# One program of four blocks: keys of the causal attention made inside the recurrence's steps

## What is computed

```python
h_t  = GRU(h_{t-1}, x_t)                       # 256 steps, h_0 = cond
q, k, v = h @ Wq + bq, h @ Wk + bk, h @ Wv + bv   # 16 heads of 128
w    = softmax(q @ k.T / sqrt(128) + causal_mask)
x1   = x + (w @ v) @ Wo + bo
# conditioned attention: 16 heads of 16
xn   = rms_norm(x1, g) * (1 + scale) + shift   # scale, shift from cond
o    = softmax(rms_norm(q2) @ rms_norm(k2).T / 4) @ v2
y    = o + o @ W_out
out  = x1 + moe_ffn(y)     # 16 experts, 4 per position, and a shared one
```

## Time and profile of the kernel before

| | |
|---|---|
| median of 3 runs | 1055.14 us (1053.57, 1055.14, 1122.17) |
| profiled execution | 1052.69 us, its span 1050.9 us |
| PE, PEld busy | 933.1 us (89%), 698.3 us |
| DVE, ACT, POOL busy | 675.3, 530.9, 538.2 us |
| granted TensorE clock, mean of the span | 0.773 |

### The profile page before, as it was taken

One profiled execution on the slowest core, in us unless ns is written; L12 is line 12 of the kernel. 1 busy time (PEld: TensorE's weight loads), 2 busy tenths in 40 slices (PEclk: granted clock), 3 DMA queues, 4 the chain that ended last, 5 costly groups with the idle time before them and its releaser, 6 DMA issues. The chain is left out here.

```text
span 1050.9 us, 33951 instructions
## 1 busy us (share of the span) xinstructions
PE 933.1 (89%) x13640; PEld 698.3 (66%) x13640; DVE 675.3 (64%) x2501; ACT 530.9 (51%) x1781; POOL 538.2 (51%) x1183
## 2 busy tenths in 40 slices
PE   3889989899898998778999999857787999999997
PEld 3777777777777777666888888634343656665664
DVE  5866666666666666677777777667682666665665
ACT  3544444444444444455777777647665333233332
POOL 1266666666666666653555555257100655655652
PEclk8555555555555555578999999989799899999999
DMA  7100000000000000020110100010000133343441
GB/s 274 43 4 3 3 3 3 4 2 4 3 4 2 4 3 3 3 85 1 32 32 32 31 32 2 2 39 1 2 1 1 46 109 105 119 128 107 121 126 41
DMA packets 12744, 40.91 MB, mean 39 GB/s; under 512 B 2070, under 2 KB 3864, under 8 KB 12204
## 3 DMA queue, kind: packets, MB, share of 16 engines
q1 hardware_dynamic: 12588, 38.74, 11.5%
HBM read 37.36 MB, written 1.11 MB: 37 GB/s over the span
## 5 line engine op out<-in xcount | busy, mean ns | idle before, releaser
L423 POOL COPY gp<-hq 128x16 f16<-128x16 f16 x256 | 69.0, 269 | 174.6 <-DVE hq L413 174.6
L306 ACT ACTIVATE r_scan<-gr 128x8 f32<-128x8 f32 x256 | 46.3, 181 | 180.3 <-PE gr L218 180.3
L218 PEld LDWEIGHTS gr<-hq,w_two 128*128 128x128 f16 x1024 | 47.3, 107 | 115.1 <-DVE hq L408 109.9
L398 DVE TENSOR_REDUCE z_sum<-gz 128x8 f32<-128x16 f32 x256 | 44.8, 175 | 121.2 <-PE gz L218 120.5
L432 POOL TENSOR_TENSOR q_part<-q_raw,q_part 128x64 f16<-128x64 f32 x238 | 111.4, 468 | 19.2
L218 PE MATMUL gr<-hq,w_one 128*128 128x4 f16 x2048 | 117.6, 166 | 0.0
L218 PE MATMUL gr<-hq,w_two 128*128 128x4 f16 x1024 | 68.6, 172 | 51.6 <-DVE hq L408 28.8
L273 PE MATMUL gq<-gp,wq_part 128*128 128x64 f16 x1428 | 114.4, 237 | 0.0
L1735 POOL TENSOR_SCALAR w_hi<-wf_ffn 128x512 f16<-128x512 f32 (+1 forms) x56 | 29.6, 529 | 162.3 <-POOLq L985 75.1
L922 POOL TENSOR_SCALAR probs<-probs,rinv 128x128 f32<-128x128 f32 (+1 forms) x128 | 52.9, 425 | 111.9 <-DVE rinv L812 111.9
L430 POOL CAST q_part<-q_raw 128x64 f16<-128x64 f32 x238 | 109.0, 458 | 0.0
(11 more groups left out here) (237 smaller groups left out, 2733.6 us busy)
## 6 DMA issues: line engine op xcount, KB each, us to landing
wf_ffn<-in_wf SPq DMA_DIRECT2D x28, 384.0 KB, 3.2
raw_attn<-in_pairs SPq DMA_DIRECT2D x8, 770.0 KB, 5.2
cw_of<-cw_rows SPq DMA_DIRECT2D x9, 512.0 KB, 3.7
shared<-in_wq SPq DMA_DIRECT2D x1, 2056.0 KB, 12.1
cw_of<-cw_rows SPq DMA_DIRECT2D x4, 448.0 KB, 3.6
cw_of<-cw_rows SPq DMA_DIRECT2D x4, 384.0 KB, 3.5
cw_of<-cw_rows SPq DMA_DIRECT2D x4, 320.0 KB, 3.6
xT<-in_xT SPq DMA_DIRECT2D x1, 1024.0 KB, 7.6
```

What stands on the lines that cost most here:

```text
L218: mm = pe.matmul(out, w[:, j, rows], src, start=False, stop=False, skip_group_check=True)
L306: nc.scalar.activation(r_scan[:, 2::3], R[bp][:, k * 8:(k + 1) * 8], ACT.Sigmoid, scale=1.0 / GS).then_inc(t_in, 1)
L423: nc.gpsimd.tensor_copy(gp[:, :, :, :, t].rearrange("p q j b -> p q (j b)"), hq[:, nxt, :, 2::3]).then_inc(h_stored, 1)
```

## The change

**Recurrence.** Wk (2 MB) and its bias are loaded after wq. In steps 8 to 23 POOL splits one head's Wk, after the copy of the state and before the queries. From step 16, each step makes the keys of one head for the 16 positions before (6 matmuls of 64 columns, L300 of after) between the products and the queries; ACT reads out the high part (`k_made`) between the tanh and `q_raw`, and DVE makes the rest after the state's low part and before the next z. After 8 steps SP writes `k_made` to a buffer in DRAM, `k_kept`, by two DMAs. DVE waits for the copy of one step earlier ahead of z, PE no longer in each step.

**Attention.** Keys are made only for the last 16 positions, once a head (6 matmuls of 64 columns); the others of each head come back from `k_kept` (480 KB, one head ahead), so that the scores' moving operand is read in runs of 16. Values come in half batches, one group of 6 matmuls in each of the first 56 units. An exponential waits only for its own half of the maxima. `oT` has three buffers, and the projection lags by three units.

**Conditioned attention.** The q/k product alternates between two banks; the turned rows of the last two tiles alternate between two banks; the banks of the scores are 3, then 4, then 5. The batch product comes after the values, and the second shifted tile earlier. The feed-forward part is unchanged. Semaphores are merged to make room, and the raw weights of the recurrence share a buffer with the split Wk.

The core of the diff:

```diff
+        raws = sb("raws", [P, 6 * J * D + J * B * T])
+        whh, wih = (raws[:, n * J * 3 * D:(n + 1) * J * 3 * D].rearrange("p (j n) -> p j n", j=J)
+                    for n in range(2))
+        xT = raws[:, 6 * J * D:6 * J * D + J * B * T].rearrange("p (j b t) -> p j b t", j=J, b=B)
+        wk_part = raws[:, 0:H1 * J * P].bitcast(FP16).rearrange("p (w h n) -> p w h n", w=2, h=H1)
...
             sp.dma_start(wq, dram["wq"]).then_inc(loaded["wq"], 16)
+            sp.dma_start(bk[:], dram["bk"]).then_inc(loaded["wk"], 16)
+            sp.dma_start(wk, dram["wk"]).then_inc(loaded["wk"], 16)
...
+            for n in range((T - QB) // KSET):
+                first = n * KSET % H1
+                sp.wait_ge(k_lo, (n + 1) * KSET)
+                for q in range(2):
+                    sp.dma_start(k_kept[first:first + KSET, :, q, n * KSET // H1, :].rearrange("h p n -> p h n"),
+                                 k_made[:, n % 2, q]).then_inc(k_out[n % 2], 16)
...
-                if t:
+                if blk and k == 0:
                     pe.wait_ge(h_stored, t)
+                if blk:
+                    n_key = t - QB
+                    if t == QB + 1:
+                        pe.wait_ge(emb_act, 4)
+                    if t < 2 * QB:
+                        pe.wait_ge(wk_ready, k + 1)
+                    if queries_before(t):
+                        pe.wait_ge(q_read, queries_before(t))
+                    elif n_key >= 2:
+                        pe.wait_ge(k_lo, n_key - 1)
+                    for j in range(J):
+                        for w, g in ((1, 0), (0, 0), (0, 1)):
+                            mm = pe.matmul(q_bank[1 - t % 2][:, B * QB:2 * B * QB]
+                                           .rearrange("p (b t) -> p b t", b=B),
+                                           wk_part[:, w, k, j * P:(j + 1) * P],
+                                           gp[:, g, j, :, (blk - 1) * QB:blk * QB],
+                                           start=(j == 0 and w == 1), stop=(j == J - 1 and g == 1))
+                    mm.then_inc(k_psum, 1)
                 if query_of(t):
                     h, c = query_of(t)
                     m = queries.index(t)
-                    if m == 0:
-                        pe.wait_ge(emb_act, 4)
+                    pe.wait_ge(k_lo, t - QB)
                     if m < H1:
                         pe.wait_ge(wq_ready, c + 1)
                     if m >= 2:
                         pe.wait_ge(q_split, m - 1)
                     for j in range(J):
                         for w, g in ((1, 0), (0, 0), (0, 1)):
-                            mm = pe.matmul(q_bank[m % 2][:, 0:B * QB].rearrange("p (b t) -> p b t", b=B),
+                            mm = pe.matmul(q_bank[t % 2][:, 0:B * QB].rearrange("p (b t) -> p b t", b=B),
...
+                if t >= QB:
+                    n_key = t - QB
+                    group, place = n_key // KSET, n_key % KSET
+                    if n_key == 0:
+                        act.wait_ge(bk_ready, 1)
+                    if place == 0 and group >= 2:
+                        act.wait_ge(k_out[group % 2], 32 * (group // 2))
+                    act.wait_ge(k_psum, n_key + 1)
+                    nc.scalar.activation(k_made[:, group % 2, 0, place, :],
+                                         q_bank[1 - t % 2][:, B * QB:2 * B * QB], ACT.Identity,
+                                         bias=bk_scaled[:, k:k + 1]).then_inc(k_hi, 1)
...
+                if t >= 2:
+                    dve.wait_ge(h_stored, t - 1)
                 dve.wait_ge(z_psum, t + 1)
...
+                if t >= QB:
+                    n_key = t - QB
+                    group, place = n_key // KSET, n_key % KSET
+                    dve.wait_ge(k_hi, n_key + 1)
+                    nc.vector.scalar_tensor_tensor(
+                        out=k_made[:, group % 2, 1, place, :], in0=q_bank[1 - t % 2][:, B * QB:2 * B * QB],
+                        scalar=bk_scaled[:, k:k + 1], in1=k_made[:, group % 2, 0, place, :],
+                        op0=ALU.add, op1=ALU.subtract).then_inc(k_lo, 1)
...
                 pool.wait_ge(h_two, t + 2)
                 nc.gpsimd.tensor_copy(gp[:, :, :, :, t].rearrange("p q j b -> p q (j b)"),
                                       hq[:, nxt, :, 2::3]).then_inc(h_stored, 1)
+                if KSPLIT <= t < KSPLIT + H1:
+                    h = t - KSPLIT
+                    if h == 0:
+                        pool.wait_ge(loaded["wk"], 32)
+                        pool.wait_ge(w_ready, 1)
+                        pool.wait_ge(inputs_ready, 4)
+                        pool.wait_ge(x_ready, B)
+                    else:
+                        pool.wait_ge(wk_ready, h)
+                    nc.gpsimd.tensor_scalar(wk_part[:, 0, h], wk[:, h], KS, 0.0, ALU.mult, ALU.add)
+                    nc.gpsimd.tensor_scalar(wk_big[:], wk[:, h], KS, 0.0, ALU.mult, ALU.add) \
+                        .then_inc(wk_written, 1)
+                    pool.wait_ge(wk_written, h + 1)
+                    nc.gpsimd.tensor_tensor(wk_part[:, 1, h], wk_big[:], wk_part[:, 0, h],
+                                            ALU.subtract).then_inc(wk_ready, 1)
+                if t == KSPLIT + H1:
+                    pool.wait_ge(wk_ready, H1)
                 if query_of(t):
                     h, c = query_of(t)
                     m = queries.index(t)
...
+        kh = sb("kh", [P, 2, 2, H1, B * QB], FP16)
...
-            return 2 * (h + 1) + b // 2 if 0 <= u < units and b % 2 == 0 and h + 1 < H1 else None
+            return h + 1 if 0 <= u < units and b == 0 and h + 1 < H1 else None
...
-            return B * (pr + 1) + 2 * e + b // 2 if 0 <= u < units and b % 2 and pr + 1 < pairs else None
+            i, pr = u % (2 * B), u // (2 * B)
+            return (pr + 1, i // TC, i % TC) if 0 <= u < units and pr + 1 < pairs else None
...
+            def load_keys(h):
+                sp.dma_start(kh[:, h % 2, :, 0:H1 - 1, :], k_kept[h][:, :, 0:H1 - 1, :]).then_inc(k_in[h % 2], 16)
+
+            sp.wait_ge(k_out[0], 16 * (T - QB) // KSET)
+            load_keys(0)
+            load_keys(1)
...
+                sp.wait_ge(s_psum, B * (h - 1))
+                load_keys(h)
...
-                                       w_part["k"][:, h // 2 % 2, w, rows],
-                                       gp[:, g, j, 2 * half:2 * half + 2, :],
+                        mm = pe.matmul(last_keys(bank).rearrange("p (b t) -> p b t", b=B),
+                                       w_part["k"][:, h // 2 % 2, w, rows], gp[:, g, j, :, T - QB:T],
...
-                                       kh[:, e, k, b, 0:(tc + 1) * P], start=(m == 0), stop=(m == 2))
+                                       kh[:, e, k].rearrange("p a (b r) -> p b a r", b=B)[
+                                           :, b, 0:(tc + 1) * P // QB, :],
...
+            for u in range(units + 3):
                 if u + 1 < units:
                     h, b, _, _ = unit(u + 1)
                     if u + 1 == B * (H1 - 2):
                         pe.wait_ge(q_split, len(left_sets))
-                    pe.wait_ge(k_ready, 2 * h + b // 2 + 1)
-                    if value_group(u - 2) is not None:
-                        pe.wait_ge(v_ready, value_group(u - 2) + 1)
-                    if key_group(u - 2) is not None:
+                    if b == 0:
+                        pe.wait_ge(k_in[h % 2], 16 * (h // 2 + 1))
+                        pe.wait_ge(k_ready, h + 1)
+                    if value_group(u - 2):
+                        pe.wait_ge(v_ready, values_to(*value_group(u - 2)))
+                    if key_group(u - 2):
                         pe.wait_ge(k_ready, key_group(u - 2) + 1)
                     scores(u + 1)
-                if u >= 2:
-                    pe.wait_ge(oT_ready, u - 1)
-                    if (u - 2) % (2 * B) == 0:
-                        pe.wait_ge(w_split["o"], splits("o", (u - 2) // (2 * B)))
-                    projected(u - 2)
+                if u >= 3:
+                    pe.wait_ge(oT_ready, u - 2)
+                    if (u - 3) % (2 * B) == 0:
+                        pe.wait_ge(w_split["o"], splits("o", (u - 3) // (2 * B)))
+                    projected(u - 3)
...
+                    if u >= 2:
+                        pe.wait_ge(oT_ready, u - 1)
...
+                if key_group(u):
+                    h = key_group(u)
+                    pe.wait_ge(least_ready, 2 * (u + 2))
+                    if h // 2:
+                        pe.wait_ge(w_split["k"], splits("k", h // 2))
+                    keys(h, S[(u + 1) % 2])
+                if value_group(u):
+                    pr, b, sc = value_group(u)
+                    pe.wait_ge(least_ready, 2 * (u + 2))
+                    pe.wait_ge(w_split["v"], splits("v", pr))
+                    values(pr, b, sc, S[(u + 1) % 2][:, 0:2 * DH1]).then_inc(v_psum, 1)
...
-                act.wait_ge(least_ready, u + 1)
```

(29 more changed lines are left out.)

367 lines of the change are left out of this document (195 added, 172 removed).

## The result

Four executions of the changed kernel have a median of 1044.91 us (1041.69 to 1046.54) against 1054.84 us before; the ratio is 0.9905, with a 95% interval from 0.988 to 0.993. One execution of the kernel before, 1122.17 us, fell in a slow state of the chip and is left out of the ratio. The change is faster by about 10 us, not by the 26 that were forecast. The profiled execution took 1041.69 us, with a span of 1039.9.

A forecast was written before the change was run, and what follows sets the result against it. It took a chain of dependent instructions to bound the recurrence and PE the attention. 1052.7 + 10 (splitting Wk) - 28 (attention) - 6 (conditioned attention) = 1028.7, so 1029 us; own range 1019 to 1040, wider range 1014 to 1046.

The forecast's parts named there:

- The keys in the steps: Recurrence, 240 steps: the keys' work on PE, ACT and DVE fits their idle time, price 0.
- Its new wait for the state's copy: Recurrence, DVE ahead of z: the wait concerns the step before last and is long met, price 0.
- Splitting Wk: Recurrence, steps 8 to 23: POOL's split of Wk lengthens these steps, +10 us (+5 to +17).
- Attention: -28: Attention: cheaper units -25, an earlier start of exponentials in the last 8 units -3; sum -28 us.
- The other case, -30: Attention, seven pairs of heads: -30 us instead of -25 if the buffers swallow the lateness from POOL's splits.
- the finer wait, -3: Attention, last 8 units: ACT waits per half of the maxima and starts some 0.35 us earlier, -3 us.
- rival D: Attention: another engine, POOL or DVE, sets the pace at 3.0 us a unit, total 1040 us; chance 0.14.
- Conditioned attention: -6: Conditioned attention: two product banks -1.3, turned copies -3.5, reordering -1; in all -6 us (-1 to -9).
- A: Recurrence: busier PE lifts the clock, -6 to -12 us, total about 1020; chance 0.12.
- B: Recurrence: the keys only nearly fit, +0.03 to +0.1 us a step, total 1036 to 1053; chance 0.14.
- C: Recurrence: the keys cost 0.107 us a matmul, +0.24 a step, +58 us, total 1087; chance 0.05.
- the forecast of faster than 2%: Whole kernel: measured below 1034 us, about 2% from no change; chance 0.60.

The follow-up runs named there:

- experiment 1: Kernel after with the two waits ahead of DVE's z sum in the other order (z_psum first, h_stored second): 1030.31 us, ratio 0.978.
- experiments 1 to 3: Order of DVE's two waits: z_psum first in after, 1030.31 us; kernel before plus the h_stored wait, written first, 1063.71 us; written second, 1054.17 us.
- experiment 7: Kernel after with each of POOL's splits of the attention's weights cut in two parts, in consecutive units: 1032.74 us, ratio 0.980.
- experiment 8: Kernel after with ACT's exponentials waiting for both halves of the maxima again: 1055.64 us, ratio 1.000.
- 10 and 12: Each step's six key matmuls issued twice: on after with swapped waits, 1029.90 us; on that plus Wk split by ACT and DVE and POOL's splits halved, 1009.67 us.

## Why the prediction was right or wrong

**The keys in the steps: 0.** Right, and for the reason given. ACT's 0.30 and DVE's 0.28 (0.32 forecast) fit; PEld's idle time in the usual step with three input projections fell from 0.40 to 0.08 (experiment 1), which is what I had left for it; in a step with two it fell from 0.51 to 0.19.

**"Its new wait for the state's copy concerns the step before last and is long met. Price 0".** This is the step that failed. It was right that the copy is long there, and wrong that a met wait is free: it took from `z_psum` its place on the z sum, and `z_psum` then cost 0.07 us more each time, 0.037 of it in the step, 9.4 us in all (experiments 1 to 3). The order of DVE's queue showed the second wait, before and after:

```order
L398 TENSOR_REDUCE z_sum<-gz 128x8 [waits z_psum]
L457 TENSOR_REDUCE z_sum<-gz 128x8 [waits z_psum,h_stored]
```

I asked only whether the added wait would be met in time, not what it does to the one beside it. With the two lines in the other order the profiled execution is 1029.1, the forecast's number, but with luck: 2.6 of it are the conditioned attention's shorter execution. Of the 12.7 us by which the profiled execution of after missed the forecast of 1029, the wait is 9.4; the rest is about the attention's 1.8, the conditioned attention's 1.1 and the split's 0.7.

**Splitting Wk: +10.** Measured, 10.7: steps 7 to 32 took 54.5 us instead of 42.9, less 0.9 that is the wait's. The sum was right by luck in its parts: without queries a step is 2.23, not 1.95 (the copy is 0.38 there, as it runs beside DVE's rest, and the scaling 0.46), and POOL excludes DVE's chain at the same time; with queries 2.19 to 2.85, not 2.95. The lower end of its range, +5, doesn't follow either: with 0.58 for the rest the sum gives 7.6.

**Attention: -28.** Measured -26.2. Eight units take 22.62 where I had 22.7, and the units with POOL's two splits are the late ones, as worked out. The other case, -30 if the lateness goes, should have been -34 by the same numbers ((26.2 - 8 x 2.67) x 7), and experiment 7 shows it: 21.37. Wrong in the sum: the finer wait, -3 in the last units alone. It is worth 10.7, since without it a loop of ACT and DVE of 2.97 us paces nearly every unit (experiment 8). So rival D (DVE between maxima and rests, 3.0 a unit) was the truth of the kernel without that part of the change; I had asked which engine is busy most, not how long the unit's loop is. In the last units the gain was 1.9.

**Conditioned attention: -6.** Measured -4.9 between two profiles and -5.9 in a run of its own. The five turned copies lie 4.6 us from first to last instead of 8.1, -3.5 as forecast.

**Rivals.** A didn't come with the change; with twelve key matmuls the clock rose (10 and 12), but that it gives time back by itself isn't shown. B named the right size (0.03 to 0.1 a step), and a wait's own cost among its causes, but as what fills a margin: the margins held, and the cost lies on the chain. C fell: the keys' matmuls come every 0.053 us.

**The numbers.** The range held the time; the forecast of faster than 2% didn't. The 9.4 us of the wait were in the range only because B was.

Not settled: why the conditioned attention takes 118.2 to 118.5 us in some executions and 115.8 to 116.8 in others with the same code, why the attention's first eight units take 30.0 to 33.6 us, and what a clock of 1.00 gives the recurrence without the doubled matmuls. The first two are seen between profiles of kernels that don't differ there.
